# A recurrence's products kept in PSUM: the scan reads them from the bank they were formed in

## The reference, cut to what matters

```python
def step(M, inp):
    q_t, k_t, v_t, g_t = inp
    M = M * decay + jnp.einsum('bhr,bhd->bhrd', g_t * k_t * scale, v_t)
    y = jnp.einsum('bhr,bhrd->bhd', q_t, M)
    return (M, y)
_, Y = jax.lax.scan(step, M0, xs)
```

## Time and profile before

| | us |
|---|---|
| median of 3 runs | 2239.45 (2238.22 to 2243.85) |
| the profiled execution's own time | 2244.34 |
| its span, first to last instruction | 2242.6 |
| busy: TensorE | 2059.3 (92%) |
| busy: VectorE | 1514.4 (68%) |
| busy: ScalarE | 1303.1 (58%) |
| busy: GpSimd | 1420.7 (63%) |
| mean granted TensorE clock | 0.963 of full speed |

### The profile page before, as it was taken

The page is one execution under the profiler, slowest core; times in us unless marked ns, Lnnn a source line. Parts: engine busy times, 40 slices in busy tenths (PEclk is TensorE's granted clock), DMA queues, the critical chain, the costliest instruction groups (busy, mean ns, idle before and its releaser), DMA issues. The chain is left out here.

```text
span 2242.6 us, 47389 instructions
## 1 busy us (share of the span) xinstructions
PE 2059.3 (92%) x19706; PEld 1502.6 (67%) x19706; DVE 1514.4 (68%) x1834; ACT 1303.1 (58%) x1574; POOL 1420.7 (63%) x671
## 2 busy tenths in 40 slices
PE   4799999999999998999999989999999767679897
PEld 3577777767777776777777767777777432234465
DVE  5666666766666667666666676666666248867768
ACT  2477767676767676776767676767676521010232
POOL 0277777777777777777777767777777635423335
PEclk8899999999999999999999999999999887769999
DMA  8010101111010113010001030101000030012221
GB/s 233 15 34 14 27 14 41 45 43 27 14 27 13 27 32 71 15 27 16 26 15 48 11 76 7 34 13 27 14 18 4 3 145 0 0 48 71 71 68 55
DMA packets 47762, 83.51 MB, mean 37 GB/s; under 512 B 7328, under 2 KB 31520, under 8 KB 46784
## 3 DMA queue, kind: packets, MB, share of 16 engines
q1 hardware_dynamic: 47552, 80.47, 13.1%
HBM read 73.70 MB, written 5.31 MB: 35 GB/s over the span
## 5 line engine op out<-in xcount | busy, mean ns | idle before, releaser
L765 POOL TENSOR_TENSOR acc<-acc,PR 128x1024 f32<-128x1024 f32 x480 | 1154.3, 2405 | 346.8 <-ACT PR L546 309.5
L621 DVE TENSOR_REDUCE amx<-ps 128x2 f32<-128x1024 f32 x512 | 626.8, 1224 | 386.5 <-PE ps L319 386.5
L546 ACT ACTIVATE PR<-ps 128x1024 f32<-128x1024 f32 x512 | 518.4, 1019 | 235.6 <-PE ps L327 235.6
L506 ACT ACTIVATE ps<-NM 128x1024 f32<-128x1024 f32 x416 | 427.2, 1028 | 189.0 <-DVE V L606 144.8
L335 PE MATMUL ps<-PR,V 128*64 128x256 f32 x4096 | 505.2, 389 | 0.1
L335 PEld LDWEIGHTS ps<-PR,V 128*64 128x64 f32 x4096 | 273.9, 138 | 163.8 <-issue 33.7
L327 PE MATMUL ps<-qh,KH 64*128 64x256 f32 x2048 | 328.3, 309 | 32.2 <-ACT ps L506 28.9
L301 PE MATMUL ps<-wv,C 64*128 64x256 f32 x4608 | 314.7, 280 | 0.0
L301 PEld LDWEIGHTS ps<-wv,C 64*128 64x128 f32 x4608 | 305.3, 187 | 8.5
L290 PE MATMUL ps<-C,wk 64*128 64x512 f32 x2304 | 310.0, 396 | 1.0 <-DVE x L655 1.0
L327 PE MATMUL ps<-ql,KH 64*128 64x256 f32 x2048 | 300.0, 279 | 0.0
(11 more groups left out here) (191 smaller groups left out, 1846.7 us busy)
## 6 DMA issues: line engine op xcount, KB each, us to landing
wk<-wk_split SPq DMA_DIRECT2D x62, 192.0 KB, 3.2
wv<-wv_split SPq DMA_DIRECT2D x30, 384.0 KB, 5.1
bc<-wm_rows SPq DMA_DIRECT2D x32, 256.0 KB, 4.3
craw<-in_ctx SPq DMA_DIRECT2D x30, 256.0 KB, 3.9
we<-in_we SPq DMA_DIRECT2D x10, 768.0 KB, 6.0
wo<-in_wo SPq DMA_DIRECT2D x68, 64.0 KB, 2.2
wq<-in_wq SPq DMA_DIRECT2D x32, 128.0 KB, 3.0
craw<-in_ctx SPq DMA_DIRECT2D x30, 128.0 KB, 3.9
```

What stands on the lines that cost most here:

```text
L506: act.activation(ps[:, first_bank:first_bank + 2, :].rearrange("p h (k n) -> p h k n", k=2), row.unsqueeze(2).to_broadcast([P, 2, 2, ROWS] ...
L546: act.activation(PR[:, pr_slot(t, hf), :, :, :].rearrange("p h k n -> p (h k n)"), ps[:, bank:bank + 2, :].rearrange("p h n -> p (h n)"), ...
L621: dve.tensor_reduce(amx[:, :, t, c], psG, AX.X, ALU.max).then_inc(g_max, 1)
L765: pool.tensor_tensor(flat(acc[:, :, :, :]), flat(acc[:, :, :, :]), flat(PR[:, pr_slot(t, hf), :, :, :]), ALU.add).then_inc(acc_done, 1)
```

## The change

The product is written back into the PSUM bank that the pair filled, in place, and the scan takes its second tensor from there. The tile kv goes, and with it VectorE's wait for its buffer. Since the bank now holds the product until the scan has read it, TensorE's wait before it fills the bank again goes from the product two steps back (kv_ready) to the scan two steps back (m_done), as does the wait ahead of the last output projection, which uses bank 0. Tiles behind kv in its region move down by its 4 KB per partition.

```diff
-        w4, bd, ..., vh, vl, kv, M, qm, yT, ow, vecs = room(
+        w4, bd, ..., vh, vl, M, qm, yT, ow, vecs = room(
...
-            ("kv", [P, 2, W], F32), ("M", [P, 2, W], F32), ("qm", [P, 4, W], F32), ("uT", [P, 2, 2, W], F32),
+            ("M", [P, 2, W], F32), ("qm", [P, 4, W], F32), ("uT", [P, 2, 2, W], F32),
...
                 if J >= 2:
-                    pe.wait_ge(kv_ready, J - 1)
+                    pe.wait_ge(m_done, J - 1)
                 pe.matmul(ps[:, J % 2, :], selvr[:, dd, :], vh[:, g, :], start=True, stop=False)
...
                 if hf == 1:
-                    pe.wait_ge([zo_added, kv_ready][i], [2, 4 * STEPS][i])
+                    pe.wait_ge([zo_added, m_done][i], [2, 4 * STEPS][i])
...
-                if J >= 2:
-                    dve.wait_ge(m_done, J - 1)
                 dve.wait_ge(vb_ps, J + 1)
-                dve.tensor_tensor(kv[:, J % 2, :], ps[:, J % 2, :], kk[:, g, :], ALU.mult).then_inc(kv_ready, 1)
+                dve.tensor_tensor(ps[:, J % 2, :], ps[:, J % 2, :], kk[:, g, :], ALU.mult).then_inc(kv_ready, 1)
                 dve.wait_ge(kv_ready, J + 1)
                 if J >= 2:
                     dve.wait_ge(qm_ready, J - 1)
-                dve.tensor_tensor_scan(M[:, J % 2, :], dect[:, g, :], kv[:, J % 2, :], 0.0, ALU.mult, ALU.add).then_inc(m_done, 1)
+                dve.tensor_tensor_scan(M[:, J % 2, :], dect[:, g, :], ps[:, J % 2, :], 0.0, ALU.mult, ALU.add).then_inc(m_done, 1)
```

More of the change, by code:

```diff
@@ L859, in tail @@
         wel = sb("wel", [P, 3, 6, DM], F32R)
-        w4, bd, rope, t1, t2, gate, selvr, dect, qr, kk, vh, vl, kv, M, qm, yT, ow, vecs = room(
+        w4, bd, rope, t1, t2, gate, selvr, dect, qr, kk, vh, vl, M, qm, yT, ow, vecs = room(
             ("w4", [P, 4, 2, DM], F32), ("bd", [P, 2, 2, 2, P], F32), ("rope", [P, 2, W], F32), ("t1", [P, 2, W], F32),
```

## The result

The changed kernel took 2226.35 us in the median of 4 runs (2224.51 to 2228.42), beside 2240.51 for the kernel before: ratio 0.9936, 95% interval 0.9921 to 0.995, 14 us or 0.64% faster. A second comparison with more runs of the kernel before gave 0.9919 (0.9901 to 0.9938); one of its six runs of the changed kernel took 8200.67 us and has no part in the ratio, the others 2218.75 to 2228.4. Forecast were 2228.7 us and -10.8.

What follows compares the result with a forecast made beforehand. VectorE was taken as the busy engine up to 1932 us, TensorE from 2013. Released scan holds, less what the later wait gives back, came to 6.4 us, then 4.4 among the experts: -10.8 from 2239.45, 2228.7 us; range 2222 to 2238.

Steps and rivals of the forecast that it cites:

- Part 1: VectorE's scans reading terms from PSUM: none held by GpSimd, 1.226 instead of 1.595 us each, up to 23.6 us less.
- The surcharge in the Trainium skill: Rival's rule, PSUM source dearer: 65 ns more per scan, 4.1 us, time about 2232 to 2233; rival's chance 0.10.
- Part 2: VectorE's product writing to PSUM: 0 extra taken, bounds 0 and 0.14 us for each of 64, 9.0 us.
- Part 3: VectorE's product no longer waits on the scan two back: 0 taken, gain under 2 us.
- Part 4: TensorE fills a bank after scan J-2: every fourth step's scan-pair-sum-qm-scan loop stalls 0.8 us at high clock, 2.15 at low.
- the rival in which nothing else was left: Rival: scans stay held, only TensorE's later wait acts, +8 us, 2247.5; chance 0.08.
- A low-clock group: Four recurrence steps with TensorE at 1.2 GHz: 10.07 us before, 9.55 forecast after.
- the forecast's terms: Later wait's costs if scans stay held: +1.2, +1.0, +1.15, +1.8, +1.7, +1.0 at steps 6, 14, 26, 30, 34, 44.
- The scans' waits for qm: VectorE's idling ahead of scans, 15.7 us before: to remain only at steps 6, 10, 14, ... and 23.
- One sign of being wrong: The prediction would be wrong if TensorE waits for scans elsewhere than at every fourth step.
- The sum by stretches: Recurrence walked through step by step: 4.1 us saved at step 34, 6.4 by 2013 us, then 4.4 of TensorE's idling among experts.
- more comes back: Rival: shorter idling before the shared expert's output keeps TensorE's clock up, 2.9 us more, likewise elsewhere; 2223 to 2226; chance 0.10.

Runs made afterwards that it cites:

- the steps in SBUF: Changed kernel with the product of every odd step written to a two-buffer SBUF tile and scanned from there; ratio 0.9947 to the kernel before.
- late wait alone: Kernel before with only the pair of step J waiting for scan J-2 instead of product J-2, product and scan staying in SBUF; ratio 1.0043.
- changed, second: The changed kernel measured again, unaltered, with a second profile, against the kernel before; ratio 0.9919.
- the late wait with eight slots: Kernel before with the pair waiting for scan J-2 and eight qm slots instead of four, kv still in SBUF; ratio 0.9895.
- the bias-later kernel: Changed kernel with GpSimd's second pair of bias additions behind step 35 instead of step 20, four qm slots; ratio 0.9932.
- the ring: Kernel before with eight qm slots instead of four and nothing else, kv still in SBUF; ratio 0.9902, 22 us faster.

## Why the prediction was right, by its own steps

**Part 1, right.** No scan is held, 78.1 us for the group, 79 forecast. That PSUM does not make the scan dearer held too: 1.221 us against 1.226 from SBUF, 5 ns less, between the 0 that was taken and the lower bound of -20 ns. That lower bound had weak ground: the earlier trace rows show only two instructions with both tensors in SBUF. Over the whole trace before, the twelve of that form that meet no GpSimd instruction take 727 to 747 ns and the 32 with a tensor in PSUM 721 to 751, so there is no difference either way. The surcharge in the Trainium skill, "VectorE: DVE Perf Modes", errata-adjusted cycle table, does not appear in the scan; here the measurement decides. The exclusive hold is what the Trainium skill, "SBUF — State Buffer", states under "Who interferes with whom" for two SBUF inputs beside a GpSimd instruction that reads SBUF, and the trace agrees, in the two forms of the scan in one program.

**Part 2, right within 0.013 us.** The product takes 687 instead of 674 ns, 0.8 us over all 64.

**Part 3** was not measured alone; the steps in SBUF above show that the holds do not go with that wait.

**Part 4, right in its mechanism.** Its price alone is 9.6 us, 8 forecast for the rival in which nothing else was left. A low-clock group, from scan 26 to scan 30, became 0.5 us shorter in both profiles of the changed kernel, as forecast (10.07 to 9.55). By steps, the start of each scan less the first scan's, minus the same before:

| scan of step | 6 | 14 | 18 | 22 | 26 | 30 | 34 | 51 | 63 |
|---|---|---|---|---|---|---|---|---|---|
| late wait alone | +1.1 | +2.5 | +3.8 | +6.0 | +7.1 | +8.8 | +11.3 | +10.4 | +10.3 |
| changed | +0.5 | -0.8 | -0.4 | -0.4 | -1.2 | -1.7 | -1.6 | -6.7 | -13.2 |
| changed, second | -0.3 | -1.4 | -2.7 | -2.8 | -3.6 | -4.0 | -5.3 | -10.1 | -16.6 |

The late wait adds 1.1 to 2.5 us from column to column up to step 34: 11.3 us there, where the forecast's terms come to 6.9. Step 22, which it had left out, adds 2.2 and step 18, for which it had "a little", 1.4. At step 44, where it had 1.0, nothing is added, and 1.0 comes back by the end. So the total of 8 came near the measured price partly by luck, and a few us of it are the grain of the clock. The scans' waits for qm are at 14 places: at most of every fourth step and, besides, at step 23 (4.0 us), as forecast, and at step 63 (0.4), which was there before (0.6).

One sign of being wrong did show by its letter: TensorE waits for scans elsewhere than at every fourth step. Its pairs have 20 idle times that "DVE M" ended, 15 of them at other steps, 34.6 us over all 20. The sign was badly chosen. Before, they had 19 that "DVE kv" ended, 14 at other steps, 33.2 us over all, and the late wait with eight slots shows that the later wait costs nothing there.

**The sum by stretches.** Until the start of scan 35, 4.1 us were forecast; the two profiles have 2.2 and 5.9. From there to scan 51, just ahead of the shared expert's output, 2.3 were forecast, and 4.5 and 4.1 found. From scan 51 to the sum of ranks behind step 63 it is 7.5 us for the 4.4 forecast: that sum starts 14.2 us sooner from the first scan than before, step 51's scan 6.7. Of it, TensorE's idling among the experts went from 5.2 us to 1.0, 4.2 saved for 4.4.

**What was mis-sized** is the term of TensorE's clock. The sum took it at nothing and left it to the rival "more comes back", chance 0.10. The 16 matmuls of the shared expert's output took 6.49 us before and 3.69 in both profiles after: 2.8 us, the rival's 2.9. The late wait alone, whose idle time ahead of them is 3.79 us as before, has 6.33:

```profile
2025.30 6.33 PE L1101 MATMUL ps<-sw,zT 128*128 128x256 f32 x16 [3.79 <-issue]
```

and seven of the eight other kernels, with 1.0 to 2.8 us of idling ahead, have 3.69; the bias-later kernel, 2.81 idle, has 5.32. The shared expert's third product, 5.59 before, takes 4.32 and 4.37 after, another 1.2. -10.8 - 2.8 - 1.2 = -14.8 us, beside a measured -14 and -18. That this meets the first so well is in part luck: the stretch up to scan 35 came out 1.9 us under its forecast in one profile and 1.8 over it in the other. The forecast and this rival were not exclusive, as they should not have been set up: the first held and the second came on top. That the shorter idling is what kept the clock up fits eleven of the twelve profiles; it was not isolated, and why the bias-later kernel differs stays open.

The range, 2222 to 2238, held both medians (2226.35 and 2228.11).

## What to carry to other kernels

When a VectorE group's mean is well above its own minimum, look at whether its long instructions end a fixed time after a GpSimd instruction did (here 1.08 us, all 31 of them): then they are held, and are not slow work. Compare the forms that read two SBUF tensors with those that read one SBUF tensor and PSUM, and leave an operand in the PSUM bank where it was formed if TensorE can wait for the bank. Reading two tensors is not the only way to be held: the tensor_scalar of the earlier trace rows reads one and took 1.14 us, while another of the same shape took 0.17. Then follow the buffer that stays occupied longer all the way round its ring: here the later wait cost 10 us through four slots of another tile, and nothing with eight. When a transfer of slots releases several instructions at once, count the burst's holds as well as the wait; the ring was worth 22 us before any operand moved.

## What the hardware showed that I had not expected

VectorE multiplies a PSUM bank in place, 128x512 in float32, at 687 ns beside 674 with SBUF as destination. GpSimd gains too: its slowest product of the recurrence took 2.21 us before, beside a scan, and takes 1.72 after, with 1.27 in the median. The two slowest that are left (1.70 and 1.72) ran beside the experts' `t<-t,be,bc`, which reads two SBUF tensors and is still held: in the changed kernel 17 of its 32 take 1.3 to 1.8 us, where it takes 0.72 to 0.75 with GpSimd idle. Whether that reaches the end was not tested. And one and the same program, at the same place, had TensorE's projection at 3.17 and at 1.88 us in two executions, 1.3 of the 3 us by which their recurrences differ.
